# Bias and residual adds moved from POOL-issued DMAs to POOL arithmetic, and a weight fold moved from ACT to DVE

## The reference

```python
x = x + 0.5 * ffn(layernorm(x))       # quantised 512x512 weight plus LoRA; ffn adds a bias row
h = layernorm(x)
r = rmsnorm(h, ln1_w)
h2 = h + mamba2(r)                    # projections, conv of 4 taps, chunked scan (16 chunks of 128), w_out
x = x + h2 + (silu(rms(h2)*ln2_w @ gate_w.T) * (rms(h2)*ln2_w @ up_w.T)) @ down_w.T
x = x + 0.5 * ffn(layernorm(x))
```

## Time and profile before

| what | value |
|---|---|
| median of the three runs | 830.73 us |
| time of the profiled execution | 830.73 us |
| its span (first to last instruction) | 829.0 us |
| mean granted TensorE clock | 0.977 of full speed |
| busy: PE, DVE, ACT, POOL | 770.8, 640.4, 434.9, 336.8 us |
| DMAs issued by POOL | 16 for the bias, 16 for the residual, 88 for the MLP's output |

### The profile page before, as it was taken

The page is one execution under the profiler, slowest core; times in us unless marked ns, Lnnn a source line. Parts: engine busy times, 40 slices in busy tenths (PEclk is TensorE's granted clock), DMA queues, the critical chain, the costliest instruction groups (busy, mean ns, idle before and its releaser), DMA issues.

```text
span 829.0 us, 10802 instructions
## 1 busy us (share of the span) xinstructions
PE 770.8 (93%) x3560; PEld 358.9 (43%) x3560; DVE 640.4 (77%) x1245; ACT 434.9 (52%) x853; POOL 336.8 (41%) x389
## 2 busy tenths in 40 slices
PE   7987799999999798989879899999999999996998
PEld 3433355454455344444334344444444444442343
DVE  4889768968867876777798797897879877756884
ACT  2685556766675655534434546455655456433431
POOL 4523343552432256557733125225234243223554
PEclk9998999999999999999999999999999999999899
DMA  8932533452521214120070253554553734431554
GB/s 298 203 77 57 104 81 76 82 110 53 88 52 28 38 26 114 39 51 1 0 153 13 51 140 64 108 123 87 128 90 63 163 67 77 76 69 34 134 145 127
DMA packets 98167, 72.41 MB, mean 87 GB/s; under 512 B 67984, under 2 KB 75152, under 8 KB 98112
## 3 DMA queue, kind: packets, MB, share of 16 engines
q0 software_dynamic: 17280, 31.46, 21.5%
q1 hardware_dynamic: 80448, 40.15, 18.5%
q10 hardware_dynamic: 384, 0.10, 0.1%
HBM read 20.32 MB, written 4.19 MB: 30 GB/s over the span
## 4 chain that ended last, share of the span: by engine, by line
PE 51%; DVE 5%; ACT 2%; DMA 1%; POOL 1%; issue 1%; SPq 0%; ACTq 0%; DVEq 0%; POOLq 0%
PE PS L1850 47%; PE PS L1978 2%; DMA raw_d<-down_t 1%; PE PS L1968 0%; DVE raw L1446 0%; ACT raw_gu L989 0%; DVE xs L1788 0%; DMA raw_gu<-n_p 0%; DVE xs L1711 0%; PE PS L1943 0%; DVE mk L1387 0%; DVE raw L1447 0%; DVE n L1443 0%; ACT w_in L1037 0%; DVE pre L1694 0%
## 5 line engine op out<-in xcount | busy, mean ns | idle before, releaser
L678 POOL DMA_DIRECT2D xs<-x x59 | 51.5, 878 | 156.9 <-ACT x L1076 153.4
L1850 PE MATMUL PS<-h,w_in 128*128 128x512 f16 x480 | 109.0, 380 | 1.6 <-DMA h<-hn_p 1.4
L1850 PE MATMUL PS<-h,x_t 128*128 128x512 f16 x408 | 95.7, 384 | 3.1 <-DVEq L1418 3.1
L1850 PEld LDWEIGHTS PS<-h,w_in 128*128 128x128 f16 x480 | 46.8, 98 | 66.6 <-issue 15.6
L1850 PE MATMUL PS<-n_T,stage 128*128 128x512 f16 x288 | 71.5, 379 | 4.1 <-DVE xs L1788 2.3
L485 POOL TENSOR_TENSOR r<-mv,mhalf 128x1 f32<-128x1 f32 (+1 forms) x32 | 28.3, 883 | 91.1 <-DVE mv L1198 71.9
L1850 PEld LDWEIGHTS PS<-h,x_t 128*128 128x128 f16 x408 | 39.9, 99 | 53.2 <-issue 5.1
L1076 ACT ACTIVATE x<-PS,d_d 128x512 f32<-128x512 f32 x59 | 40.1, 679 | 42.3 <-PE PS L1850 36.4
L678 POOL DMA_DIRECT2D xs<-n x29 | 26.1, 899 | 70.1 <-ACT n L1076 69.1
L1850 PE MATMUL PS<-w_ffn,raw_gu 128*128 128x512 f16 x192 | 45.6, 394 | 7.5 <-DMA raw_gu<-n_p 7.5
L1046 ACT ACTIVATE xds<-tm,dgh 128x512 f32<-128x512 f32 x24 | 17.3, 722 | 62.0 <-DVE tm L1775 62.0
(11 more groups left out here) (311 smaller groups left out, 1816.1 us busy)
## 6 DMA issues: line engine op xcount, KB each, us to landing
xs<-x POOLq DMA_DIRECT2D x75, 256.0 KB, 3.3
xs<-n POOLq DMA_DIRECT2D x29, 256.0 KB, 3.3
x_t<-x_in SPq DMA_DIRECT2D x16, 256.0 KB, 3.6
x_t<-hb POOLq DMA_DIRECT2D x16, 256.0 KB, 4.9
out<-x_t SPq DMA_DIRECT2D x16, 256.0 KB, 2.3
raw_gu<-gate_t SPq DMA_DIRECT2D x7, 512.0 KB, 4.2
raw_gu<-up_t SPq DMA_DIRECT2D x7, 512.0 KB, 5.2
raw_d<-down_t SPq DMA_DIRECT2D x7, 512.0 KB, 5.9
```

What stands on the lines that cost most here:

```text
L678: po.dma_start(chunk_of(xs, c), d_tmps[d % 3], accum_op=ALU.add).then_inc(s_acc[d % 3], 16)
L1850: ins = pe.matmul(out_, lhs(a, b, k), rhs(a, b, k), start=first and n == 0, stop=last and n == len(todo) - 1)
```

## The change

Three edits.

1. `xb` no longer issues a DMA: POOL computes `x_t + hb` itself with a `tensor_tensor` of 128x512 float32, and raises `e_x_bias`. The wait for the DMA two before goes. DVE waits for `e_x_bias`.
2. `rms2` likewise adds `x2` to `xs` with a `tensor_tensor` and raises `e_xres`; all the waits on the old semaphores are turned into waits on it, and the counts of `added` lose the term for the residual.
3. ACT's `fold` goes. DVE multiplies both halves by `ln2` with two `tensor_tensor` of 128x1024 in step 8, and takes all three maxima in step 9, so that nothing of it is left in step 7.

```diff
             def xb(c, j):
                 po.wait_ge(e_n0_hi, c + 1)
-                if c >= 2:
-                    po.wait_ge(*biased(c - 2))
-                po.dma_start(x_t[:, j, :], hb[:, :], accum_op=ALU.add).then_inc(s_xb[c % 2], 16)
+                po.tensor_tensor(x_t[:, j, :], x_t[:, j, :], hb[:, :], ALU.add).then_inc(e_x_bias, 1)
...
                 po.wait_ge(e_x2, c + 1)
-                po.dma_start(chunk_of(xs, c), x2[:, j % 2, :], accum_op=ALU.add).then_inc(s_acc[c % 2], 16)
+                po.tensor_tensor(chunk_of(xs, c), chunk_of(xs, c), x2[:, j % 2, :], ALU.add).then_inc(e_xres, 1)
...
-            def fold(g):
-                if g == 0:
-                    ac.wait_ge(s_raw, 48)
-                for k in range(KB):
-                    last = ac.activation(raw_gu[:, g, k, :], raw_gu[:, g, k, :], ACT.Copy, scale=ln2[:, k:k + 1])
-                last.then_inc(e_fold, 1)
...
-                if c in (2 * CH - 2, 2 * CH - 1):
-                    fold(c - (2 * CH - 2))
...
             def x1_stats(c, j, b):
                 ve.wait_ge(e_ffn, c + 1)
-                ve.wait_ge(*biased(c))
+                ve.wait_ge(e_x_bias, c + 1)
...
-                    ve.wait_ge(*x2_added(c - 2))
+                    ve.wait_ge(e_xres, c - 1)
...
-            def maximum_gu(g):
-                ve.wait_ge(e_fold, g + 1)
-                return ve.tensor_reduce(mx3[:, g:g + 1], raw_gu[:, g, :, :], mybir.AxisListType.XY, ALU.max, apply_absolute_value=True)
+            def fold():
+                ve.wait_ge(s_raw, 48)
+                lnb = ln2[:, :].unsqueeze(2).broadcast_to([P, KB, PAIR])
+                for g in range(2):
+                    link(ve.tensor_tensor(raw_gu[:, g, :, :], raw_gu[:, g, :, :], lnb, ALU.mult), e_fold, g + 1)
+
+            def maxima_gu():
+                for g in range(2):
+                    ve.tensor_reduce(mx3[:, g:g + 1], raw_gu[:, g, :, :], mybir.AxisListType.XY, ALU.max, apply_absolute_value=True)
...
-                if c == 2 * CH - 1:
+                if c == 2 * CH:
+                    fold()
+                if c == 2 * CH + 1:
+                    maxima_gu()
                     maximum_d()
-                if c == 2 * CH:
-                    maximum_gu(0)
-                if c == 2 * CH + 1:
-                    maximum_gu(1).then_inc(e_max, 1)
```

More of the change, by code:

```diff
@@ L252, in build @@
         s_acc = [sem(f"s_acc{k}") for k in range(3)]
-        s_xb = [sem(f"s_xb{k}") for k in range(2)]
         s_cT = [sem(f"s_cT{k}") for k in range(NC)]
@@ L259, in build @@
         e_aexp = sem("e_aexp"); e_sel = sem("e_sel"); e_wf = sem("e_wf"); e_dve = sem("e_dve"); e_pool = sem("e_pool")
-        e_x_bn, e_x_var, e_x_rstd, e_x_scale, e_n0_hi, e_n0_lo, e_n0_tr = (
-            sem(n) for n in "e_x_bn e_x_var e_x_rstd e_x_scale e_n0_hi e_n0_lo e_n0_tr".split())
+        e_x_bn, e_x_var, e_x_rstd, e_x_scale, e_x_bias, e_n0_hi, e_n0_lo, e_n0_tr = (
+            sem(n) for n in "e_x_bn e_x_var e_x_rstd e_x_scale e_x_bias e_n0_hi e_n0_lo e_n0_tr".split())
         e_n0T, e_ffn, e_x1, e_x1_bn, e_x1_var, e_rms1, e_hn_scale = (
@@ L275, in build @@
             sem(n) for n in "e_x2 e_ssq e_ms e_rms2 e_h2_hi e_h2_lo".split())
-        e_h2T, e_ncs, e_gu, e_tanh_g, e_silu_g, e_gated, e_gated_hi = (
-            sem(n) for n in "e_h2T e_ncs e_gu e_tanh_g e_silu_g e_gated e_gated_hi".split())
+        e_h2T, e_xres, e_ncs, e_gu, e_tanh_g, e_silu_g, e_gated, e_gated_hi = (
+            sem(n) for n in "e_h2T e_xres e_ncs e_gu e_tanh_g e_silu_g e_gated e_gated_hi".split())
         e_T, e_thi, e_tlo, e_norm, e_sadd, e_add, e_dn, e_ev, e_p1, = (
@@ L355, in tile_down @@
             return e_down, (i + 1) * CH
[L357 to L361, removed]
         def added(d):
-            return s_acc[d % 3], 16 * (d // 3 + 1 + (NCH // 2 if d % 3 < 2 else 0))
+            return s_acc[d % 3], 16 * (d // 3 + 1)
         def d_bank(d):
@@ L671, in x_add @@
                 if p == 0:
-                    po.wait_ge(*x2_added(c))
+                    po.wait_ge(e_xres, c + 1)
                 elif (p - 1, c) in DOWNS:
@@ L1073, in evict @@
                 else:
-                    ac.wait_ge(*x2_added(NCH - 2))
-                    ac.wait_ge(*x2_added(NCH - 1))
+                    ac.wait_ge(e_xres, NCH)
                 ac.activation(d_tmps[d % 3], bank(d_bank(d)), ACT.Copy, scale=d_d[:, p % 3:p % 3 + 1]).then_inc(e_ev, 1)
@@ L1374, in silu_z @@
                 ve.scalar_tensor_tensor(szs[i % 2][:, h, :], th[:, 1, :], 1.0, bank(PLAN["proj", i, CB + h][0]), ALU.add, ALU.mult).then_inc(e_sz, 1)
-            def maximum_gu(g):
-                ve.wait_ge(e_fold, g + 1)
-                return ve.tensor_reduce(mx3[:, g:g + 1], raw_gu[:, g, :, :], mybir.AxisListType.XY, ALU.max, apply_absolute_value=True)
+            def fold():
[6 more added lines that the diff above has]
+                    ve.tensor_reduce(mx3[:, g:g + 1], raw_gu[:, g, :, :], mybir.AxisListType.XY, ALU.max, apply_absolute_value=True)
             def maximum_d():
-                ve.wait_ge(s_raw, 48)
-                ve.tensor_reduce(mx3[:, 2:3], raw_d[:, :, :], mybir.AxisListType.XY, ALU.max, apply_absolute_value=True)
+                ve.tensor_reduce(mx3[:, 2:3], raw_d[:, :, :], mybir.AxisListType.XY, ALU.max, apply_absolute_value=True).then_inc(e_max, 1)
             def bound_g(p, g):
```

## The result

The changed kernel is slower: 833.97 us median (830.36 to 835.25) against 828.93 us (826.74 to 832.30) for the kernel before on the same chip. The ratio is 1.0052, 95% interval [1.0039, 1.0065], which is +4.3 us (+3.2 to +5.4); the prediction had +7.0. The ratio with its interval is what counts in this document; it compares all executions of both kernels and isn't the quotient of the two medians, which are 5.0 us apart. One execution of experiment 1 (917.02 us, granted clock 0.842) was in a slower state and isn't in its ratio. The profiled execution's span is 833.6 us, where it was 829.0.

A forecast was written before the change was run, and what follows sets the result against it. PE, with hardly a gap from about 102 us, was taken as the bound, a DVE, POOL and ACT loop in the prologue; 1.6 + 3.1 − 0.7 + 2.1 + 0.9 = 7.0 us on 830.73 gave 837.7 us, range 830.0 to 841.5.

The forecast's parts named there:

- A (cover holds): Rival: DVE's lateness vanishes in existing waits, only the three maxima reach PE; 831.2 us, up to 834; chance 0.26.
- meetings: POOL adds delaying DVE taps: bias 0.70 us, residual 0.85 us in steps 1 and 5; residual 0.88 us in step 10.
- C (more): Rival: POOL's next small instruction takes the port too, fold leaves 1.3 us, clock costs 1.7; 842.3 us; chance 0.16.
- B (faster): Rival: without bias DMAs the prologue's transposes land sooner, saving 3.8 us of PE waits; 826.2 us; chance 0.10.
- prologue: Bias adds on POOL delay DVE's taps in the prologue's chunk loop, 0.72 and 0.7 us among them; +1.6 us.
- steps 1, 2, 5, 6: Bias and residual adds delay DVE taps in steps 1 and 5, so PE loses 1.55 us each time; +3.1 us.
- fold off ACT, step 8: ACT loses the fold group ahead of the exponential, closing PE's 0.71 us wait at 248.09; 0.7 us gained.
- three maxima, residual, steps 9 and 10: Three maxima make a tap 1.2 us late; step 10's residual add delays another by 0.88; +2.1 us.
- clock, step 10: PE's longer idle times of 3.4 and 2.7 us lower the granted clock; +0.9 us, bounds 0 and 1.7.
- MLP's entry: POOL's MLP work moves 0.4 to 0.6 us per later step, taken by DVE's later waits; no cost counted.

The follow-up runs named there:

- experiment 1: Kernel before with only the third edit (fold and maxima on DVE), both DMAs kept: ratio 1.0001 [0.9984, 1.0017].
- experiment 10: Kernel before with only the bias adds of chunks 0 to 7 on POOL's arithmetic, all other bias and residual adds still DMAs: ratio 1.0002 [0.9982, 1.0022].
- experiment 8: Changed kernel with filler matmuls in step 10, 10 before the exponential's wait and 20 before the row's: ratio 1.0043 [1.0028, 1.0059] to the kernel before.
- experiment 9: Changed kernel with the residual add ahead of the mean in `rms2` and 20 filler matmuls before step 10's exponential wait: 1.0042 [1.0024, 1.0061] to the kernel before.
- experiment 12: Kernel before, DMAs kept, fold on ACT in steps 3 and 6, maxima in 4, 7, 8, `bound_spread(0)` later: ratio 0.9997; with 10 fillers 0.9988.
- experiment 3: Kernel before with only the first edit, the bias add on POOL: ratio 1.0028 [1.0008, 1.0047], +2.3 us.
- experiment 2: Kernel before with only the second edit, the residual add on POOL: ratio 1.0076 [1.0056, 1.0096], +6.3 us.
- experiment 7: Changed kernel with the residual add moved ahead of the mean in `rms2`: ratio 1.0026 [1.0009, 1.0043] to the kernel before.

## Why the prediction was right in direction and too high in size

The mechanism was right: POOL's adds hold up DVE's two-input instructions, narrow adds take the loss away, and another slot for the add takes its part away. A (cover holds) is refuted in the steps, where all four meetings and the one of step 10 reached PE; C (more) too, with single taps of 1.42 us at most, though the clock did cost its 1.7 us in two of three profiles. B (faster) is refuted in its size of 3.8 us, not in its sign: with the DMAs gone and the adds narrow the prologue is 1.1 us shorter in the profiles, and the timed runs (0.7 us) neither show nor exclude that. The terms, by the means of the three profiles of each kernel:

| term | predicted | measured |
|---|---|---|
| prologue | +1.6 | 0.0 (A) |
| steps 1, 2, 5, 6 | +3.1 | +2.3 |
| fold off ACT, step 8 | −0.7 | −0.7 |
| three maxima, residual, steps 9 and 10 | +2.1 | +1.8 |
| clock, step 10 | +0.9 | +1.3 |
| MLP's entry | none | +0.2 |
| sum | 7.0 | 4.9 (timed runs: 4.3, 3.2 to 5.4) |

**The step that failed is the prologue's.** I wrote that DVE gets to its `lo0` first, so that POOL waits for it and then holds up the tap by 0.72 us, in a loop that hands all of it to PE, and I took the rest of the loop over unchanged from the trace of before. It isn't unchanged.

First, in the changed kernel POOL is there before DVE, and the reason lies 3 us earlier. POOL's small shift for the layer norm (L488, now L481, two columns) starts almost together with a tap of DVE. In all three profiles of before the shift starts 0.01 to 0.02 us ahead of the tap, stands still behind it, and takes 0.80 or 0.81 us; in all three of the changed kernel it starts 0.03 to 0.04 us ahead and takes 0.27. So ACT begins its normalisation 0.56 us sooner (67.03 for 67.59) and ends `n_p` at 70.01 instead of 70.53, when DVE is still at its previous instruction. The Trainium skill ("SBUF — State Buffer", section "Who interferes with whom") says that issue order decides which of the two blocks. At the add, where POOL leads by 0.22 us, the trace agrees: `lo0` stands still. At the shift the recorded starts are too close to give the order: at a lead of 0.01 to 0.02 us the one that was recorded first is the one that stood still. Why the lead differs between the kernels isn't known.

Second, the sooner scale is a gain that the prediction put at nothing. The narrow adds, where the shift takes 0.27 us too, have it alone: 10.30 and 10.85 us per chunk instead of 10.82 and 11.36. Against them the full adds cost 0.71 and 0.69, which is the 0.72 and 0.7 of the prediction; against the kernel before, only 0.19 and 0.18 are left (11.01 and 11.54). That the gain comes from the scale and not from transposes that land sooner is my reading: `x1_stats` starts behind DVE's own instruction each time, with no wait. Experiment 10 has one chunk in the order that I predicted, without the gain, and its add cost 0.38.

Third, the clock, which I hadn't counted here. PE's and ACT's timelines of the changed kernel:

```profile
95.56 4.31 PE L1835 MATMUL PS<-h,w_in 128*128 128x512 f16 x12
```
```profile
101.27 1.14 ACT L778 ACTIVATE Ld<-PS,ncs 128x128 f32<-128x128 f32 x4 [0.61 <-PE PS L1912]
```

At chunk 7 DVE is 0.23 us late (95.44 for 95.21), but PE's first row of step 0 is 0.93 late (102.46 for 101.53): the low clock of 96 to 100 us made the product 4.31 us long instead of 2.75, ACT waited 0.61 us for PE, and PE then for ACT. In return the first steps run at full clock, which they do in one profile of before out of three: from that row to the wait of step 2 it is 40.08 us, where it was 41.55, 40.08 and 41.59. Set against the kernel before, the terms are +1.4 for the meetings, −1.1 for the shorter loop, +0.7 for the clock ahead of the row and −1.0 for the clock behind it. Together 0.0, and +0.2 in experiment 10; that they cancel is luck. That the clock would still fall there with yet another placement of the edits isn't known: with the bias alone A is 79.92 us.

**The meetings** were 0.51 and 0.66 us instead of 0.70 and 0.85. Their number and places were right (B, and the waits of 0.88 and 1.48). The 1.27 less the lead counts from POOL's recorded start to its end, but the tap's own last part after it is only 0.55 us long instead of 0.75: 0.2 us of each meeting is start-up that passes while it stands still. Four times 0.2 is the 0.8 us by which this term was too high. In step 10 the tap is 0.66 us late for 0.88, and PE 0.74.

**The fold** went as written: the two multiplications took 3.42 us for both (one beside a POOL instruction of 2.18), inside the bounds of 2.4 and 5.0, and reached nothing.

**The clock** was my least trusted term, and came out at 1.69 us in two executions and 0.17 in one, against 0 to −0.2 before. Its cause, the longer waits, isn't shown. For it: in the eight profiles without fillers in which PE waited 3.22 us for the exponential or 2.58 for the row, the clock fell in step 10 each time, and in the three profiles with fillers never (experiments 8, 9 and 12). Against it: with the 2.19 and 1.84 us of before it fell in three profiles out of six too (the second of before, and experiments 3 and 10).

What stays open: the timed ratios of experiments 2, 3 and 9 are 4.0, 1.3 and 2.3 us above the sum of their shifted waits (for 9 that sum is 1.2 us). In the profile of experiment 2 that is clock, 1.7 us in step 10 and 2.4 in the prologue; that of experiment 3 has more clock than its timed runs; that of experiment 9 is of one of its faster executions (830.73 us, median 831.81) and doesn't show the 2.3. Why the clock falls at 87 us in some builds and at 96 or 100 in others I can't say.

## What to carry to other kernels

Before an add of 1.3 us on POOL replaces a DMA, look in DVE's timeline for the next instruction with two SBUF inputs: that is where it costs. Put the add where DVE reads PSUM, reduces or waits; the same add cost about 2 us less one slot earlier. Don't take the order of two engines at one semaphore over from the trace of before when they are within 0.3 us, and don't take over the loop around them either: what the change removes can make it shorter. A version of the change that keeps every instruction and semaphore but does next to no work (here the adds of 8 columns) separates the two. A change worth 1 us or less in a kernel whose clock falls in places can't be judged from one profile: compare stretches between fixed rows, which repeat within 0.02 us where the clock is whole.

## What the runs showed of the hardware

- A tap on DVE that stands still behind POOL ends 0.55 us after POOL's recorded end, against the 0.75 us that it takes alone (138.39 after 137.84, 144.09 after 143.54, and 72.94 after 72.39 in experiment 10).
- POOL's add takes longer too when DVE is first: 1.44 us in the prologue, 1.77 in experiment 10 and 1.81 in experiment 7, against 1.26 alone.
- Recorded starts don't say who stands still when they are hundredths apart: a POOL instruction of 128x2 took 0.27 us with a lead of 0.03 to 0.04 us on DVE's tap, and 0.80 to 0.83 us with one of 0.01 to 0.03.
- The length of what stands still doesn't matter: 128x48 took 1.21 us beside `scan_c`, and 0.21 without it.
- A reduction on DVE doesn't stand still: two of 128x1024 took 2.33 us from 275.29 beside POOL's `scan_d` (275.45, 1.27 us), and one alone 1.21. Nor does an instruction with an input in PSUM: 0.69 us at 100.69, beside 1.26 on POOL at 100.88.
- In the six profiles of the two kernels, between 90 and 300 us, the granted clock of a stretch of 4 us fell to 0.54 to 0.73 behind idle times of PE from 2.15 to 3.22 us, but not behind each of them, and in the same kernel not always at the same place; in experiment 3 it fell behind 0.69 us. In step 10 a fall cost 0.2 us when a wait of PE's followed it and 1.7 when none did; in the prologue 0.7 and 1.5.
